# Products with V in pairs of key tiles, a fused minimum that writes to its own PSUM bank, and small rows shared

## The chip, the cores and the metric

The kernel runs on one core of a Trainium2 chip. The metric is the device time of one execution, in microseconds (us). Its engines work in parallel, each on its own queue in program order, and wait for one another through semaphores: TensorE (PE; weight loads are listed apart, as PEld), VectorE (DVE), ScalarE (ACT), GpSimd (POOL) and SyncE (SP), which issues the DMAs here.

## The reference

A transformer layer over x of shape (4, 512, 512), in fp32:

```
q, k, v = x Wq', x Wk', x Wv'            # 32 query heads, 8 key/value heads, 16 wide
q, k    = rope(q), rope(k)
attn    = softmax(causal(q k' / 4))      # each key/value head serves 4 query heads
x1      = layernorm(x + (attn v) Wo')
W       = mean_w + mean(|w - mean_w|) * sign(w - mean_w)     # for w1, w2, w3
out     = layernorm(x1 + (silu(x1 W1') * (x1 W3')) W2')      # 1792 wide inside
```

## The kernel before, in words

Four batches are four sections of eight steps; a step works on one key/value head with its four query heads, a *group*. A fifth section has only the tail of the last batch's groups. Then comes the feed-forward part, a loop over pairs of weight tiles, which no edit touches. Each engine has its own written-out order of the same steps.

A step is pipelined over groups. In eleven units n = 0 to 10, TensorE does the first pass of the step's own group (`pass1`, line 1056: logits with queries on the partitions, into one of three PSUM banks), and VectorE takes from each the least of the negated, masked logits (`maxima`, line 820: one fused instruction per head and query tile, and an accumulator read; 16 pairs a group). That instruction also has an elementwise result, which nothing reads; it goes to the tile `masked` in SBUF, in bf16. GpSimd splits the maxima in three bf16 parts, TensorE transposes them (line 1063), and a DMA puts them as extra rows under the queries.

Two steps later the group has its second pass (`pass2`, lines 1073 and 1075: logits again, now with keys on the partitions, less the maximum and with the mask added; two PSUM banks), and ScalarE takes the exponential of each unit into `Pt` (line 609). Units 0 to 3 are key tile 0 (one head each, 512 queries), 4 to 7 tile 1 (384 queries), 8 and 9 tile 2 (two heads each, 256), unit 10 tile 3 (four heads, 128).

The products with V (`pv`, line 1083) take one key tile at a time: for each of four heads a matmul with 128 rows and 32 columns of stationary V, in its own quarter of the array's columns and of one PSUM bank, in fp32, which the chip runs as two instructions; so 8 matmuls a product and four products a group, all accumulating in the bank BANK_O. Their places: tile 0 behind unit 6 and tile 1 behind unit 9 of the group's second pass, tile 2 behind unit 0 and tile 3 behind unit 2 of the next step. `Pt` has two buffers; tile t uses buffer t % 2. So the exponentials of a tile wait until the product of two tiles before is done (`pv_done`, line 608), and for tile 0 that is tile 2 of the group before, behind unit 0 of the same step. ScalarE copies the finished sums out behind unit 4 (`o_copy`, line 616), and tile 0 of the next group waits for that copy.

Between the units stand pieces of other work in TensorE's order: projections of q, k and v in six of eight steps (behind units 3, 5, 7 and 8, lines 969 to 971), the output projection of the batch before, transposes. VectorE has the rope products, the copy of the transposed maxima, residuals and layernorm statistics in the same way; in the last step of a section ScalarE takes square roots for the layernorm between unit 7 and unit 8, which loads another table and then the exponential's again. SP issues its DMAs in a fixed order with waits.

Small tiles: `mkw` (zeros, then a causal mask block), `mp` (128 columns for the parts of the maxima, 48 in use), `den` and `inv` (softmax sums and their reciprocals), `onesf` (128 x 128 ones for one column sum ahead of the feed-forward part, line 1146).

Of the kernel before, what the change touches and what calls it, by code (L numbers as in the profile page):

```python
# [27 lines left out]
F32 = mybir.dt.float32  # L28
F32R = mybir.dt.float32r
BF16 = mybir.dt.bfloat16  # L30
# [128 lines left out]
def layer(nc, xt, x, wqkv, wo, wall, cos, sin, ident, identf, mask, out):  # L159
    with ExitStack() as top:  # L160
# [75 lines left out]
        asum = top.enter_context(nc.sbuf_tensor("asum", [P, 3, NCO], F32))  # L236
        few = top.enter_context(nc.sbuf_tensor("few", [P, 6, QT], F32))
        csum, coef, sd, mean, shift, rs = (few[:, n] for n in range(6))
        onesf = top.enter_context(nc.sbuf_tensor("onesf", [P, P], F32))
        bnst = top.enter_context(nc.sbuf_tensor("bnst", [P, QT, 6], F32))  # L240
        mv = top.enter_context(nc.sbuf_tensor("mv", [P, QT, 2], F32))

# [12 lines left out]
        with ExitStack() as ctx:  # L255
            def sb(name, shape, dt):
                return ctx.enter_context(nc.sbuf_tensor(name, shape, dt))
# [1 line left out]
            NC = NH * HD + 2 * NKV * HD  # L259
            NM = 3 * GH * QT  # L260
            woH, woL = sb("woH", [P, KT, D], F32R), sb("woL", [P, KT, D], F32R)
            idb, mkw = sb("idb", [P, P], BF16), sb("mkw", [P, S], BF16)
            mk = mkw[:, S - P:S]
            Oe = sb("Oe", [P, S], F32)
            Oc = sb("Oc", [P, KT, S], F32)
            den, inv = sb("den", [P, 2 * GH * S // P], F32), sb("inv", [P, 2 * GH * S // P], F32)
            Inv = sb("Inv", [P, S], F32)
            OH, OL = sb("OH", [P, KT, S], F32R), sb("OL", [P, KT, S], F32R)
            negM = sb("negM", [P, 2, GH, QT], F32)
            mp_all = sb("mp", [P, P], BF16)  # L270
            mp = mp_all[:, 0:NM].rearrange("p (a h t) -> p a h t", a=3, h=GH)
            mT = sb("mT", [NM, P], BF16)
            with ExitStack() as first:


                def sb1(name, shape, dt):
                    return first.enter_context(nc.sbuf_tensor(name, shape, dt))

                wqH, wqL = sb1("wqH", [P, KT, NC], F32R), sb1("wqL", [P, KT, NC], F32R)
                xH, xL = sb1("xH", [P, KT, S], F32R), sb1("xL", [P, KT, S], F32R)  # L280
                xraw = sb1("xraw", [P, 2, S], F32)
                cs, sn = sb1("cs", [P, S], F32), sb1("sn", [P, S], F32)
                vT = sb1("vT", [P, S], F32)
                masked = sb1("masked", [P, 3, S], BF16)
                rp = sb1("rp", [P, 2, S], F32)
                co = sb1("co", [P, 2, 2, 512], F32)
                parts = sb1("parts", [P, 3, S], BF16)
                Qs, Ks = sb1("Qs", [P, NH, S], BF16), sb1("Ks", [P, NKV, S], BF16)
                Pt = sb1("Pt", [P, 2, GH, S], F32)
                V = sb1("V", [P, QT, NKV, 2 * HD], F32)  # L290
            XH, XL = sb("XH", [P, KT, B, S], F32R), sb("XL", [P, KT, B, S], F32R)

# [25 lines left out]
            with nc.Block() as block:  # L318
# [235 lines left out]
                def _(act):  # L554
# [48 lines left out]
                    def exp_unit(g, n):  # L603
                        t, h, m = U2[n]
                        w = S - P * t
                        act.wait_ge(p2_done, g[0] * NU + n + 1)
                        if h == 0:
                            act.wait_ge(pv_done, g[0] * QT + t + 1)
                        act.activation(Pt[:, t % 2, h:h + m, P * t:S],  # L609
                                       PS[:, BANK_P2 + (g[1] * NU + n) % 2, 0:m * w].rearrange("p (m w) -> p m w", m=m),  # L610
                                       ACT.Exp, scale=SCALE).then_inc(exped, 1)

                    def o_copy(g):
                        act.wait_ge(pv_done, g[0] * QT + QT + 2)
                        act.wait_ge(o_kept, g[0] * 16 + 16)
                        act.activation(Oe[:], PS[:, BANK_O, :], ACT.Copy).then_inc(o_out, 1)

# [71 lines left out]
                def _(dve):  # L689
# [124 lines left out]
                    def maxima(g, n):  # L814
                        t, h, m = U1[n]
                        w = P * (t + 1)
                        dve.wait_ge(p1_done, g[0] * NU + n + 1)
                        for i in range(m):
                            bank = PS[:, BANKS_P1[(g[1] * NU + n) % 3], i * w:(i + 1) * w]
                            least = dve.tensor_tensor_reduce(masked[:, (g[1] * NU + n) % 3, i * w:(i + 1) * w], bank,  # L820
                                                             mkw[:, S - w:S], -1.0, -MASKED,
                                                             ALU.add, ALU.min, negM[:, g[1] % 2, h + i, t:t + 1])
                        least.then_inc(p1_free, 1)

# [113 lines left out]

                    dve.memset(V[:], 1.0).then_inc(ready0, 1)
                    dve.memset(Ks[:], 1.0).then_inc(ready0, 1)  # L940
                    dve.memset(mp_all[:], 0.0).then_inc(ready0, 1)
                    dve.memset(onesf[:], 1.0).then_inc(ready0, 1)
                    dve.memset(mkw[:, 0:S - P], 0.0)
                    for ring in (g_free, exped, pv_done, co_abs, h_out):
                        dve.sem_inc(ring, 2)
                    for ring, free in ((p1_free, 3), (o_out, 1), (o_norm, 1), (o_kept, 16), (max_in, 16), (o_split, 4),
                                       (y_free, 16)):
                        dve.sem_inc(ring, free)
                    for k in range(KT):
# [16 lines left out]
                def _(pe):  # L966
# [93 lines left out]
                    def max_transpose(g, use):  # L1060
                        pe.wait_ge(max_split, g[0] + 1)
                        pe.wait_ge(g_free, use[0] + 1)
                        pe.transpose(g_bank(use[1]).bitcast(BF16)[:, 0:P], mp_all[:], idb[:]).then_inc(g_done, 1)

                    def pass2(g, n):
                        t, h0, m = U2[n]
# [8 lines left out]
                            last = pe.matmul(bank[:, i * w:i * w + P], mk, idb[:], start=False, stop=True)  # L1075
                        last.then_inc(p2_done, 1)

                    def pv(g, t):
                        if t == 0:
                            pe.wait_ge(o_out, g[0] + 1)  # L1080
                        pe.wait_ge(exped, g[0] * NU + LAST2[t] + 3)
                        for h in range(GH):
                            last = pe.matmul(PS[32 * h:32 * (h + 1), BANK_O, P * t:S], V[:, t, g[1], :],  # L1083
                                             Pt[:, t % 2, h, P * t:S], start=(t == 0), stop=(t == QT - 1),
                                             tile_position=(0, 32 * h))
                        last.then_inc(pv_done, 1)

                    def project_out(b, t, use, k):
                        if k == 0:
# [9 lines left out]
                    def section(sec):  # L1099
                        b = sec.b  # L1100
                        for st in range(NKV):
# [10 lines left out]
                            for n in range(NU):  # L1112
                                if g1:
                                    pass1(g1, n)
                                if g2:
                                    pass2(g2, n)
                                if n == 0 and g3:
                                    pv(g3, 2)
                                if n == 2 and g3:
                                    pv(g3, 3)  # L1120
                                if n in PROJECT_AT and up:
                                    tile, who = PROJECT[st]
                                    project(b + (who == "nxt"), tile, up, PROJECT_AT.index(n))
                                if not sec.cur and st < 2 and n in (2, 4, 6, 8):
                                    m = 4 * st + n // 2 - 1
                                    if m == 0:
                                        pe.wait_ge(p1_free, B * NKV * NU + 3)
                                        pe.wait_ge(x1_out, (B - 1) * QT)
                                    turn_early(m)
                                if n == 6 and g2:  # L1130
                                    pv(g2, 0)
                                if n == 9 and g2:
                                    pv(g2, 1)
                                if n == 9 and sec.use("turn", st):
                                    v_use = sec.use("project", 0)[0]
                                    turn(TURN[st], sec.use("turn", st), v_use)
                                if out_use:
                                    for k in ({1: (0,), 2: (1,), 3: (2, 3)} if st == 7 else {7: (0,), 9: (1,), 10: (2, 3)}
                                              ).get(n, ()):
                                        project_out(b - 1, st - OUT_STEP, out_use, k)  # L1140
                                if n == 3 and sec.use("max", st):
                                    max_transpose(sec.behind(st, 1), sec.use("max", st))
                            if not sec.cur and st == 1:
                                pe.wait_ge(fchain, 1)
                                pe.wait_ge(t_out, 2 * KT)
                                pe.matmul(PS[:, 0, 0:3], onesf[:], csum[:, 0:3], start=True, stop=True).then_inc(coef_ps, 1)
                            if not sec.cur and st == 2:
                                pe.wait_ge(coef_out, 1)
                                for n in range(2 * KT, 3 * KT):
# [74 lines left out]
```

## Time and profile before

| | us |
|---|---|
| three runs | 999.96, 1001.02, 1001.56 (median 1001.02) |
| the profiled execution, its own time | 1000.05 |
| its span, first to last instruction | 998.2 |
| attention: the products with V, first to last start | 75.3 to 494.8 |
| feed-forward, the steady stretch | 540 to 985 |

The profile is of one execution. A line of its groups gives busy time and the mean duration of one instruction; the span of a matmul overlaps its neighbour's, so the pace is read from start to start. `x8` stands for eight merged instructions. Idle time in brackets is that in front of an instruction on its engine, with what ended it.

### The profile page before, as it was taken

To read this page: it belongs to the slowest core of one execution; us is meant where nothing else is said; L and a number is where in the kernel's file an instruction comes from. 1 tells how busy PE (TensorE), PEld (TensorE's weight loads), DVE (VectorE), ACT (ScalarE), POOL (GpSimd) and SP (SyncE) were. 2 spreads that over 40 slices of the span, in tenths; PEclk is the share of its full clock that TensorE was granted. 3 is DMA by queue.
4 is the path that set the end of the run, shared out by engine and by line. 5 is a ranking of instruction groups with operands and counts; after the bars stand their busy time and mean duration, and the time that the engine had idled before them with its cause. 6 is when DMAs were issued, how large, how long until landed. Compare 5 with 4: busy or idle time off the path is not lost.

```text
span 998.2 us, 15539 instructions
## 1 busy us (share of the span) xinstructions
PE 906.2 (91%) x5186; PEld 609.8 (61%) x5186; DVE 720.9 (72%) x1896; ACT 356.5 (36%) x681; POOL 259.7 (26%) x323
## 2 busy tenths in 40 slices
PE   4379989899999989999897999999999999999993
PEld 2134435455444545444475888888888888888882
DVE  7587756767676767767467678777877787778777
ACT  0126756655765565655822011111111111111133
POOL 2046444754356432421333010111011101110000
PEclk9579989999998999999998999999999999999997
DMA  5757776754567541511341010111101110110004
GB/s 173 99 159 166 215 191 217 180 153 122 140 175 186 147 98 54 108 54 45 119 149 64 1 64 15 49 63 63 43 20 63 63 63 0 63 63 0 1 11 158
DMA packets 49692, 95.28 MB, mean 95 GB/s; under 512 B 11424, under 2 KB 25760, under 8 KB 48608
## 3 DMA queue, kind: packets, MB, share of 16 engines
q1 hardware_dynamic: 49632, 94.53, 33.7%
q8 instruction: 32, 0.52, 0.2%
q14 instruction: 28, 0.23, 0.1%
HBM read 66.72 MB, written 14.02 MB: 81 GB/s over the span
## 4 chain that ended last, share of the span: by engine, by line
PE 73%; DVE 10%; DMA 5%; issue 3%; ACT 3%; SPq 3%; POOL 2%; ACTq 0%; DVEq 0%; POOLq 0%
PE PS L969 19%; PE PS L970 18%; PE PS L971 18%; PE PS L1083 6%; PE PS L1056 5%; PE PS L1073 5%; DVE masked L820 3%; DMA Qs<-parts 2%; PE PS L1075 2%; DMA o_dram<-Oe 1%; SPq L349 1%; ACT Pt L609 1%; POOL xL L497 1%; DVE y L724 1%; DVE rp L812 1%
## 5 line engine op out<-in xcount | busy, mean ns | idle before, releaser
L820 DVE CUSTOM_DVE_ANT_0 masked<-PS,mkw 128x384 bf16<-128x384 f32 (+3 forms) x512 | 230.3, 485 | 111.7 <-PE PS L1056 108.4
L609 ACT ACTIVATE Pt<-PS 128x512 f32<-128x512 f32 (+1 forms) x352 | 192.0, 561 | 146.1 <-PE PS L1075 121.9
L969 PE MATMUL PS<-XH,WH 128*128 128x512 f32 x448 | 176.4, 394 | 3.8 <-DVE XL L774 3.8
L970 PE MATMUL PS<-XL,WH 128*128 128x512 f32 x448 | 176.1, 393 | 0.0
L971 PE MATMUL PS<-XH,WL 128*128 128x512 f32 x448 | 175.7, 392 | 0.0
L562 ACT ACTIVATE sg<-PS 128x512 f32<-128x512 f32 x56 | 33.6, 600 | 384.3 <-PE PS L971 384.3
L1056 PE MATMUL PS<-Ks,Qs 96*128 96x384 bf16 (+3 forms) x512 | 135.4, 319 | 28.0 <-DMA Qs<-parts 15.0
L1073 PE MATMUL PS<-Qs,Ks 99*128 99x256 bf16 (+3 forms) x512 | 142.7, 312 | 14.9 <-ACT Pt L609 12.2
L724 DVE TENSOR_TENSOR y<-PS,y 128x512 f32<-128x512 f32 x224 | 138.8, 682 | 0.0
L469 POOL TENSOR_TENSOR Wr<-Wr 128x512 f32<-128x512 f32 x42 | 54.5, 1326 | 319.0 <-DMA Wr<-wall 319.0
L1056 PEld LDWEIGHTS PS<-Ks,Qs 96*128 96x128 bf16 x512 | 42.8, 101 | 127.1 <-DVE negM L820 68.9
L1083 PE MATMUL PS<-Pt,V 128*32 128x512 f32 (+3 forms) x1024 | 101.6, 470 | 0.8 <-ACT Pt L609 0.3
L1075 PE MATMUL PS<-idb,mkw 128*128 128x128 bf16 x512 | 101.9, 224 | 0.0
L969 PEld LDWEIGHTS PS<-XH,WH 128*128 128x128 f32 x448 | 85.0, 190 | 22.2 <-DVE XL L774 4.4
L970 PEld LDWEIGHTS PS<-XL,WH 128*128 128x128 f32 x448 | 85.1, 190 | 17.7
L971 PEld LDWEIGHTS PS<-XH,WL 128*128 128x128 f32 x448 | 85.1, 190 | 17.7
L713 DVE TENSOR_TENSOR hf<-PS,hb 128x512 f32<-128x512 f32 x56 | 38.7, 692 | 71.7 <-PE PS L971 71.6
L969 PE MATMUL PS<-WH,hH 128*128 128x512 f32 x224 | 87.4, 390 | 2.0 <-issue 1.1
L971 PE MATMUL PS<-WH,hL 128*128 128x512 f32 x224 | 87.3, 390 | 0.0
L970 PE MATMUL PS<-WL,hH 128*128 128x512 f32 x224 | 87.2, 390 | 0.0
L502 POOL TENSOR_TENSOR co<-co 128x512 f32<-128x512 f32 x42 | 54.2, 1292 | 67.5 <-DMA co<-wall 67.4
L1073 PEld LDWEIGHTS PS<-Qs,Ks 99*128 99x128 bf16 x512 | 51.4, 101 | 33.0 <-ACT Pt L609 26.5
(101 smaller groups left out, 1228.7 us busy)
## 6 DMA issues: line engine op xcount, KB each, us to landing
co<-wall SPq DMA_DIRECT2D x42, 512.0 KB, 5.3
Wr<-wall SPq DMA_DIRECT2D x42, 512.0 KB, 4.8
Qs<-parts SPq DMA_DIRECT2D x96, 128.0 KB, 3.9
o_dram<-Oe SPq DMA_DIRECT2D x32, 256.0 KB, 2.8
xraw<-xt SPq DMA_DIRECT2D x16, 256.0 KB, 4.1
Oc<-o_dram SPq DMA_DIRECT2D x16, 256.0 KB
y<-x SPq DMA_DIRECT2D x4, 1024.0 KB, 8.9
Inv<-inv_dram SPq DMA_DIRECT2D x16, 256.0 KB
```

Source lines behind the costliest of these rows:

```text
L469: pool.tensor_tensor(w[:, 0], w[:, 0], w[:, 1], ALU.subtract).then_inc(w_diff, 1)
L502: pool.tensor_tensor(co[:, c % 2, 0], co[:, c % 2, 0], co[:, c % 2, 1], ALU.subtract).then_inc(co_diff, 1)
L609: act.activation(Pt[:, t % 2, h:h + m, P * t:S], PS[:, BANK_P2 + (g[1] * NU + n) % 2, 0:m * w].rearrange("p (m w) -> p m w", m=m), ACT.Exp ...
L724: dve.tensor_tensor(yt, PS[:, BANK_Y + t, :], yt, ALU.add).then_inc(y_free, 1)
L820: least = dve.tensor_tensor_reduce(masked[:, (g[1] * NU + n) % 3, i * w:(i + 1) * w], bank, mkw[:, S - w:S], -1.0, -MASKED, ALU.add, ALU.m ...
L969: pe.matmul(dst, stH, moH, start=(k == 0), stop=False)
L970: pe.matmul(dst, stH, moL, start=False, stop=False)
L971: return pe.matmul(dst, stL, moH, start=False, stop=(k == n - 1))
L1056: last = pe.matmul(bank[:, i * w:(i + 1) * w], Qs[0:ROWS, GH * g[1] + h0 + i, P * t:P * (t + 1)], Ks[0:ROWS, g[1], 0:w], start=True, stop= ...
L1073: pe.matmul(bank[:, i * w:(i + 1) * w], Ks[0:ROWS + 3, g[1], P * t:P * (t + 1)], Qs[0:ROWS + 3, GH * g[1] + h0 + i, P * t:S], start=True, ...
L1075: last = pe.matmul(bank[:, i * w:i * w + P], mk, idb[:], start=False, stop=True)
L1083: last = pe.matmul(PS[32 * h:32 * (h + 1), BANK_O, P * t:S], V[:, t, g[1], :], Pt[:, t % 2, h, P * t:S], start=(t == 0), stop=(t == QT - 1 ...
```

## The change

- `pv` takes two key tiles a call: tiles 0 and 1 behind unit 9, tiles 2 and 3 behind unit 2 of the next step. It waits once, for the last exponential of the second tile.
- `Pt` becomes four buffers, one per key tile, as wide as the tile needs. The exponentials of a tile now wait for the product of the same tile in the group before (`pv_done` starts at 4 in place of 2).
- The fused minimum writes its elementwise result back to the PSUM columns that it reads, as fp32; `masked` is gone.
- `inv` is `den`: the reciprocal is taken in place. `mp` and `mkw` share one row `row`, cleared by one memset (two before). `onesf` is one column, read 128 times over.

```diff
-        onesf = top.enter_context(nc.sbuf_tensor("onesf", [P, P], F32))
+        onesf = top.enter_context(nc.sbuf_tensor("onesf", [P, 1], F32))
...
-            idb, mkw = sb("idb", [P, P], BF16), sb("mkw", [P, S], BF16)
+            idb, row = sb("idb", [P, P], BF16), sb("row", [P, NM + S], BF16)
+            mp_all, mkw = row[:, 0:P], row[:, NM:NM + S]
...
-            den, inv = sb("den", [P, 2 * GH * S // P], F32), sb("inv", [P, 2 * GH * S // P], F32)
+            den = sb("den", [P, 2 * GH * S // P], F32)
+            inv = den
...
-                masked = sb1("masked", [P, 3, S], BF16)
...
-                Pt = sb1("Pt", [P, 2, GH, S], F32)
+                Pt = [sb1(f"Pt{t}", [P, GH, S - P * t], F32) for t in range(QT)]
...
-                        act.activation(Pt[:, t % 2, h:h + m, P * t:S],
+                        act.activation(Pt[t][:, h:h + m, :],
...
-                        act.wait_ge(pv_done, g[0] * QT + QT + 2)
+                        act.wait_ge(pv_done, g[0] * QT + 2 * QT)
...
-                            least = dve.tensor_tensor_reduce(masked[:, (g[1] * NU + n) % 3, i * w:(i + 1) * w], bank,
-                                                             mkw[:, S - w:S], -1.0, -MASKED,
+                            least = dve.tensor_tensor_reduce(bank, bank, mkw[:, S - w:S], -1.0, -MASKED,
                                                              ALU.add, ALU.min, negM[:, g[1] % 2, h + i, t:t + 1])
...
-                    dve.memset(mp_all[:], 0.0).then_inc(ready0, 1)
+                    dve.memset(row[:, 0:NM + S - P], 0.0).then_inc(ready0, 1)
                     dve.memset(onesf[:], 1.0).then_inc(ready0, 1)
-                    dve.memset(mkw[:, 0:S - P], 0.0)
-                    for ring in (g_free, exped, pv_done, co_abs, h_out):
+                    for ring in (g_free, exped, co_abs, h_out):
...
-                    def pv(g, t):
-                        if t == 0:
+                    def pv(g, t0):
+                        if t0 == 0:
                             pe.wait_ge(o_out, g[0] + 1)
-                        pe.wait_ge(exped, g[0] * NU + LAST2[t] + 3)
-                        for h in range(GH):
-                            last = pe.matmul(PS[32 * h:32 * (h + 1), BANK_O, P * t:S], V[:, t, g[1], :],
-                                             Pt[:, t % 2, h, P * t:S], start=(t == 0), stop=(t == QT - 1),
-                                             tile_position=(0, 32 * h))
-                        last.then_inc(pv_done, 1)
+                        pe.wait_ge(exped, g[0] * NU + LAST2[t0 + 1] + 3)
+                        for t in (t0, t0 + 1):
+                            for h in range(GH):
+                                last = pe.matmul(PS[32 * h:32 * (h + 1), BANK_O, P * t:S], V[:, t, g[1], :],
+                                                 Pt[t][:, h, :], start=(t == 0), stop=(t == QT - 1),
+                                                 tile_position=(0, 32 * h))
+                            last.then_inc(pv_done, 1)
...
-                                if n == 0 and g3:
+                                if n == 2 and g3:
                                     pv(g3, 2)
-                                if n == 2 and g3:
-                                    pv(g3, 3)
...
-                                if n == 6 and g2:
+                                if n == 9 and g2:
                                     pv(g2, 0)
-                                if n == 9 and g2:
-                                    pv(g2, 1)
...
-                                pe.matmul(PS[:, 0, 0:3], onesf[:], csum[:, 0:3], start=True, stop=True).then_inc(coef_ps, 1)
+                                pe.matmul(PS[:, 0, 0:3], onesf[:].broadcast_to([P, P]), csum[:, 0:3], start=True, stop=True).then_inc(coef_ps, 1)
```

## Rows read from the trace of the kernel before

**Rows 1.** The page: busy us, share of the span and instructions of each engine.

```profile
PE 906.2 (91%) x5186; PEld 609.8 (61%) x5186; DVE 720.9 (72%) x1896; ACT 356.5 (36%) x681; POOL 259.7 (26%) x323
```

**Rows 2.** The chain of waits that ended last: shares of the span by line.

```profile
by line: PE PS L969 18.6%; PE PS L970 17.7%; PE PS L971 17.7%; PE PS L1083 6.3%; PE PS L1056 5.3%; PE PS L1073 4.7%; issue 3.1%; DVE masked L820 2.7%; DMA Qs<-parts 2.2%; PE PS L1075 1.9%; DMA o_dram<-Oe 1.2%; SPq L349 1.1%; ACT Pt L609 1.0
```

**Rows 3.** Windows: stretch, length; busy of PE, PEld, DVE, ACT, POOL; clock, DMA, GB/s.

```profile
179.00:291.00 112.00, 104.71 (x772) 53.55 (x768) 79.39 (x305) 70.23 (x142) 56.70 (x74) 0.97 0.60 154
...
540.00:985.00 445.00, 439.53 (x1928) 362.99 (x1928) 336.26 (x568) 61.74 (x104) 42.10 (x35) 0.99 0.11 40
```

**Rows 4.** Timeline of PE around three products: start us, us, instruction.

```profile
203.36 0.22 PE L1075 MATMUL PS<-idb,mkw 128*128 128x128 bf16 x1
203.42 0.33 PE L1056 MATMUL PS<-Ks,Qs 96*128 96x384 bf16 x1
...
204.91 0.22 PE L1075 MATMUL PS<-idb,mkw 128*128 128x128 bf16 x1
205.06 1.07 PE L1083 MATMUL PS<-Pt,V 128*32 128x512 f32 x8
206.06 0.39 PE L1056 MATMUL PS<-Ks,Qs 96*128 96x512 bf16 x1
...
210.16 0.85 PE L1083 MATMUL PS<-Pt,V 128*32 128x384 f32 x8
210.95 0.49 PE L969 MATMUL PS<-woH,OH 128*128 128x512 f32 x1
...
229.58 0.64 PE L1083 MATMUL PS<-Pt,V 128*32 128x256 f32 x8
230.15 0.39 PE L1056 MATMUL PS<-Ks,Qs 96*128 96x256 bf16 x2
```

**Rows 5.** Timeline of the weight loads of one product, merged.

```profile
205.06 0.16 PEld L1083 LDWEIGHTS PS<-Pt,V 128*32 128x32 f32 x8 [0.21 <-issue]
```

**Rows 6.** The page's groups: count, busy us, mean ns, idle before and its releaser.

```profile
L820 DVE CUSTOM_DVE_ANT_0 masked<-PS,mkw 128x384 bf16<-128x384 f32 (+3 forms) x512 | 230.3, 485 | 111.7 <-PE PS L1056 108.4
...
L1083 PE MATMUL PS<-Pt,V 128*32 128x512 f32 (+3 forms) x1024 | 101.6, 470 | 0.8 <-ACT Pt L609 0.3
```

**Rows 7.** Waits of the whole span: total us, times, longest.

```profile
ACT Pt L609 <- PE PS L1083: 21.4, 16, 4.0
```

**Rows 8.** Timeline behind the product of tile 2 at 229.58, PE and ACT.

```profile
230.35 1.74 ACT L609 ACTIVATE Pt<-PS 128x512 f32<-128x512 f32 x3 [1.42 <-PE PS L1083]
...
230.38 0.38 PE L1073 MATMUL PS<-Qs,Ks 99*128 99x512 bf16 x1
...
230.66 0.38 PE L1056 MATMUL PS<-Ks,Qs 96*128 96x256 bf16 x2
...
231.00 0.39 PE L1073 MATMUL PS<-Qs,Ks 99*128 99x512 bf16 x1
```

**Rows 9.** Timeline of DVE and of ACT at unit 7, behind tile 0's product.

```profile
236.85 0.69 DVE L820 CUSTOM_DVE_ANT_0 masked<-PS,mkw 128x512 bf16<-128x512 f32 x1 [0.87 <-PE PS L1056]
...
237.08 0.49 ACT L609 ACTIVATE Pt<-PS 128x384 f32<-128x384 f32 x1 [1.05 <-PE PS L1075]
```

**Rows 10.** Timeline of PE in front of unit 10's second pass, a section's last step.

```profile
258.48 0.23 PE L1073 MATMUL PS<-Qs,Ks 99*128 99x128 bf16 x1 [1.77 <-ACT Pt L609]
```

**Rows 11.** Groups by line and shape of VectorE: busy us, mean ns, idle before.

```profile
L820 DVE CUSTOM_DVE_ANT_0 masked<-PS,mkw 128x512 bf16<-128x512 f32 x128 | 87.3, 690 | 77.8 <-PE PS L1056 76.2
...
L700 DVE SCALAR_TENSOR_TENSOR Wr<-Wr,few 128x512 f32<-128x512 f32 x42 | 32.3, 768 | 0.0
...
L820 DVE CUSTOM_DVE_ANT_0 masked<-PS,mkw 128x128 bf16<-128x128 f32 x128 | 29.5, 287 | 11.9 <-PE PS L1056 11.8
...
L808 DVE TENSOR_TENSOR rp<-PS,cs 128x512 f32<-128x512 f32 x20 | 13.8, 688 | 5.0 <-DMA Qs<-wo 2.6 <-POOL parts L493 2.2
...
L862 DVE TENSOR_TENSOR rp<-rp,parts 128x512 f32<-128x512 f32 x3 | 2.1, 693 | 9.5 <-ACT parts L597 9.5
```

**Rows 12.** Timeline of VectorE at the start: the memsets of mp and mkw.

```profile
6.18 0.11 DVE L941 MEMSET mp<- 128x64 uint32 x1
...
6.42 0.22 DVE L943 MEMSET mkw<- 128x192 uint32 x1
```

More of the change, by code:

```diff
@@ L269, in layer @@
             negM = sb("negM", [P, 2, GH, QT], F32)
-            mp_all = sb("mp", [P, P], BF16)
             mp = mp_all[:, 0:NM].rearrange("p (a h t) -> p a h t", a=3, h=GH)
@@ L940, in _ @@
                     dve.memset(Ks[:], 1.0).then_inc(ready0, 1)
-                    dve.memset(mp_all[:], 0.0).then_inc(ready0, 1)
+                    dve.memset(row[:, 0:NM + S - P], 0.0).then_inc(ready0, 1)
                     dve.memset(onesf[:], 1.0).then_inc(ready0, 1)
-                    dve.memset(mkw[:, 0:S - P], 0.0)
-                    for ring in (g_free, exped, pv_done, co_abs, h_out):
+                    for ring in (g_free, exped, co_abs, h_out):
                         dve.sem_inc(ring, 2)
-                    for ring, free in ((p1_free, 3), (o_out, 1), (o_norm, 1), (o_kept, 16), (max_in, 16), (o_split, 4),
+                    for ring, free in ((p1_free, 3), (pv_done, QT), (o_out, 1), (o_norm, 1), (o_kept, 16), (max_in, 16), (o_split, 4),
                                        (y_free, 16)):
@@ L1062, in max_transpose @@
                         pe.wait_ge(g_free, use[0] + 1)
-                        pe.transpose(g_bank(use[1]).bitcast(BF16)[:, 0:P], mp_all[:], idb[:]).then_inc(g_done, 1)
+                        pe.transpose(g_bank(use[1]).bitcast(BF16)[:, 0:P], mp_all, idb[:]).then_inc(g_done, 1)
                     def pass2(g, n):
```

## The prediction

> **What bounds the kernel now.** I read the engine totals first: TensorE is busy 91% of the span, VectorE 72% [rows 1]. Then the chain of work that ended last, by line: the feed-forward matmuls carry over half of it, and the products with V (line 1083) 6.3% [rows 2], or 62.9 of 998.2 us. Then the busy time by stage [rows 3]. In the feed-forward stretch (540 to 985 us) TensorE is busy 439.5 of 445 us, and the diff has no edit there, so that stage stays. In the steady attention stretch (179 to 291 us) TensorE is busy 104.7 of 112 us, VectorE 79.4, ScalarE 70.2. What the change is worth is decided in attention: 32 groups of heads, one group to a step.
>
> The order of TensorE's work shows what such a step loses. A product with V uses 32 of the array's columns, all other matmuls 128. Between neighbours of the 128-column kind the next matmul starts 0.06 us after one of 128 columns (203.36 to 203.42); in front of a product it takes 0.15 us (204.91 to 205.06) [rows 4]. From a product's start to the start of whatever follows it takes 1.00 us for 512 query columns, 0.79 for 384 and 0.57 for 256 [rows 4]. Those differ by 0.21 and 0.22 per 128 columns, so four times 0.213 leaves 0.15 us that does not depend on the columns. The fixed price of one product is so 0.15 + (0.15 - 0.06) = 0.24 us. There are 1024 such matmuls [rows 6], 8 to a product: 128 products, four to a group.
>
> **The pairs.** The change issues the products of key tiles 0 and 1 together behind unit 9, and those of tiles 2 and 3 together behind unit 2 of the next step. 64 of the 128 entries from and exits to the 128-column kind go. What a second product costs right behind a first no row shows. At best all of its fixed part goes (0.24 us saved). At worst only the entry goes and it keeps its own 0.15 us (0.09 saved). I take 0.18, nearer the best, because the eight weight loads of a product all lie within 0.16 us from its start [rows 5], while its first matmuls are streaming, so the second product's loads should find cover too.
>
> The Trainium skill (TensorE: Matmul & The Clock Gate, Part 3) says that a weight load overlaps running matmuls only where their row groups differ, and these products all use the same 128 rows. By that rule the saving would be the 0.09 us of the worst case and the whole sum 4 us smaller. The eight loads inside 0.16 us, under matmuls of the same rows, speak against it here.
>
> 64 x 0.18 = 11.5 us of TensorE time. Not all of it sets the end. Four products of a group take 1.00 + 0.79 + 0.57 + 0.36 (the last by the same slope) = 2.72 us, 87.0 us in 32 groups, and 62.9 of these are on the chain: 72%. 11.5 x 0.72 = **8.3 us gained**.
>
> **The four exponential buffers.** Two buffers became four, one per key tile, so the first exponential of a step no longer waits for the third product of the group before. In the trace ScalarE waits for products 16 times, 21.4 us in all [rows 7]. Its visible price on TensorE: in the step at 229 us the exponential starts at 230.35, released by the product, and unit 2's second pass then comes 0.34 us after its pair of 256-column matmuls (230.66 to 231.00), where the same pair in front took 0.23 (230.15 to 230.38) [rows 4, 8]. That is 0.11 us, 16 times: **1.8 us gained**. Upper bound 21.4 us, lower bound nothing (the buffer wait goes, the unit then waits for the exponential itself). I take 1.8, since units 1 and 2 offer about as much TensorE work as one exponential lasts.
>
> **What the moves bring forward.** Taking tile 0's product from behind unit 6 makes units 7 to 9 reach their waits 1.00 us earlier. Queued behind such a wait on TensorE are the rest of the unit, the projection matmuls and the pair itself; VectorE's maxima and ScalarE's exponentials wait for these. There is room: in front of unit 7 VectorE idles 0.87 us and ScalarE 1.05 us, both for TensorE [rows 9], so both would simply start earlier. In the last step of a section ScalarE ends the wait instead: TensorE stands 1.77 us for an exponential [rows 10]; the moved product fits into that gap. Three such gaps of up to 1.00 us against perhaps one step per section (four of them) in which unit 9 waits out the whole 1.00 us: +3 against -4 us, which I set at nothing. After the last batch there are two steps with second passes only; there the pair stands ahead of the last unit and holds up an exponential by at most the 0.79 us of tile 1. I take 0.65 twice: **1.3 us lost**. Moving tile 2's product by two units costs nothing: ScalarE's copy of the sums comes behind unit 4, later than both products. No DMA is issued elsewhere, and SP's and POOL's queues keep their order.
>
> **The minimum's result in its own bank.** 512 fused instructions, 485 ns mean [rows 6], now write 4-byte results to PSUM in place of 2-byte ones to SBUF. No VectorE row writes to PSUM. From the rows: reading PSUM or SBUF is alike for a two-operand instruction (688 and 693 ns for 512 columns), and the dearest two-operand form of that size takes 768 ns against 690 of ours [rows 11]. So a fixed extra lies between -5 and +78 ns; the far end is a rate halved by reading and writing one bank, (690 - 287) / 384 = 1.05 ns more for each of a mean of 320 columns [rows 11]: +336 ns. I take nothing, nearest to the 688/693 pair. What hides a small extra is VectorE's own idle time (0.87 us in front of unit 7).
>
> The Trainium skill (VectorE: DVE Perf Modes, The TRN2 errata) prices a VectorE instruction's fixed part at 58 cycles between SBUF operands and 120 with a PSUM source. If a PSUM destination cost the same 62 cycles, an estimate by that page is 512 x 65 ns = 33 us of VectorE time; for the source the 688 and 693 ns contradict it.
>
> **The small rows.** Shared rows, an in-place reciprocal and a one-column constant change no instruction in a loop. One memset less at the start, 0.1 to 0.2 us [rows 12], is in no term: nothing.
>
> **Sum.** 8.3 + 1.8 - 1.3 = 8.8 us. The profiled execution took 1000.05 us (span 998.2): 991.25. The median of the runs lies 0.97 us above it, 1001.02, so the forecast is **992.2 us**. By the bounds of the pair (0.09 and 0.24 us, 72%) it is 996.3 and 989.4; with all 64 on the path and the other gains, about 986.
>
> **Rivals.**
> 1. The savings only make TensorE reach its waits earlier. For it: an eighth of the steady stretch, one step, is 14.0 us, and VectorE is busy 9.9 of them [rows 3], with waits in both directions. Against it: TensorE is 93% busy there, and the two engines idle for it. A pair that keeps all of its fixed price belongs here: the change then does not do what it says. 997 to 1003 us.
> 2. A fixed extra of 78 ns on each minimum. 512 x 78 = 40 us of VectorE; the chain's share of that line is about a tenth (2.7% of 998.2 = 27 us [rows 2], of 230 [rows 6]), so 4 us at least, and 12 where units 3 to 6 of each step run out of slack: 996 to 1004 us.
> 3. The other side: reading and writing one bank halves the rate. 16 instructions of a step cost 16 x 0.336 = 5.4 us more, VectorE needs 15.3 of 14.0 us and becomes the bound; at the 93% which TensorE reaches now a step is 16.5 us, +2.5, and 32 of them +80: about 1072 us with the other gains. It decides from (14.0 - 9.9) / 16 = 0.26 us per instruction. Against it: nothing but the lack of a row.
> 4. More than the sum: the earlier units also shorten the ScalarE waits at the ends of sections. 980 to 985 us.
>
> **Chances.** Forecast 0.46 (its own range 986 to 997), rival 1 0.22, rival 2 0.15, rival 3 0.11, rival 4 0.06. A measurement of this kernel can tell 0.2%, or 2 us, from no change. Faster: 0.46 + 0.06, half of rival 1 (0.10), a quarter of rival 2 (0.04) = 0.66. Slower: rival 3, half of rival 2 and a little of rival 1 = 0.19. Same: 0.15. The range 985 to 1003 leaves out rival 3 and the ends of 2 and 4, under 0.2.
>
> **What would show it.** Pairs of tiles 0 and 1 that take 1.70 us from their start to the start of what follows (1.64 where all of the fixed price goes, 1.79 where only the entry does), pairs of tiles 2 and 3 that take 0.84; ScalarE's waits for products near zero; VectorE's minimum still 690 ns at 512 columns; the gap in front of unit 10 at the end of a section shorter; the steady stretch about 2.5 us shorter. A minimum over 0.26 us longer, or as much waiting for VectorE and ScalarE as the switches gave back, would prove it wrong.

## The result and the profile after

The changed kernel took 1008.17 us (median of four runs, 1006.44 to 1012.28) against 1001.16 for the kernel before beside it: ratio 1.0072, 95% interval 1.0053 to 1.0092. It is 7 us slower; the prediction was 992.2. The profiled run is the slowest of the four, 1012.28 us.

The engine totals answer to [rows 1]: TensorE is busy 4.5 us less, VectorE 18 us more. The 4.5 us are not the work saved, because the mean granted clock of TensorE was 0.952 here and 0.956 in the profile before.

```profile
PE 901.7 (89%) x5186; PEld 621.4 (61%) x5186; DVE 739.0 (73%) x1895; ACT 353.0 (35%) x681; POOL 258.1 (26%) x323
```

The same two windows as [rows 3]: the feed-forward stretch is as before; in attention TensorE's busy time fell by 3.3 us and VectorE's rose by 2.3. The window holds less of TensorE's work now (743 matmuls are listed, 772 before), so the 3.3 us are no saving either. From step start to step start the third section, eight steps, takes 112.92 us (112.77 before), and not about 2.5 us less, as was forecast for a stretch of that length. TensorE's granted clock was 0.5, the lower of its two levels (1.2 GHz), for 3.4 us of that section, and for 10.3 us before.

```profile
179.00:291.00 112.00, 101.43 (x743) 54.97 (x747) 81.70 (x303) 68.69 (x142) 57.31 (x73) 0.95 0.57 149
540.00:985.00 445.00, 440.26 (x1938) 364.14 (x1937) 336.60 (x556) 60.77 (x103) 46.61 (x38) 0.99 0.11 39
```

A pair of tiles 0 and 1 on TensorE (start, us):

```profile
247.70 0.22 PE L1073 MATMUL PS<-idb,row 128*128 128x128 bf16 x1
247.85 1.71 PE L1082 MATMUL PS<-Pt,V 128*32 128x512 f32 x16
249.49 0.50 PE L967 MATMUL PS<-woH,OH 128*128 128x512 f32 x1
```

and its weight loads, answering to [rows 5]:

```profile
247.85 0.16 PEld L1082 LDWEIGHTS PS<-Pt,V 128*32 128x32 f32 x8 [0.16 <-issue]
248.31 0.13 PEld L1082 LDWEIGHTS PS<-Pt,V 128*32 128x32 f32 x4 [0.30 <-issue]
248.74 0.13 PEld L1082 LDWEIGHTS PS<-Pt,V 128*32 128x32 f32 x4 [0.30 <-issue]
```

From its start to what follows, the pair takes 1.64 us (also the median of 27 at full clock); pairs of tiles 2 and 3 take 0.79. 1.64 is the prediction's figure for "all of the fixed price goes"; the 0.79 is below its 0.84, and 0.14 less than 0.57 + 0.36. The second product's eight loads lie under the first one's stream. The Trainium skill (TensorE: Matmul & The Clock Gate, Part 3) has a line that lets a load overlap running matmuls only where the row groups differ; these rows, with all loads and matmuls on the same 128 rows, contradict that line. (The paragraph at the head of the same part also lets a load go ahead when it targets the background weight buffer; whether that is so here, no row tells.) So the pairs did their part; the loss is elsewhere.

The minimum by shape (busy us, mean ns, idle before), in the changed kernel, for [rows 11]:

```profile
L820 DVE CUSTOM_DVE_ANT_0 PS<-PS,row 128x512 f32<-128x512 f32 x128 | 89.6, 708 | 66.8 <-PE PS L1054 66.4
L820 DVE DVE_READ_ACCUMULATOR2_ANT negM<- 128x1 f32 x512 | 71.0, 139 | 0.4
...
L820 DVE CUSTOM_DVE_ANT_0 PS<-PS,row 128x128 f32<-128x128 f32 x128 | 33.4, 323 | 9.0 <-PE PS L1054 8.8
```

and the accumulator's read in the kernel before, which the prediction did not look at:

```profile
L820 DVE DVE_READ_ACCUMULATOR2_ANT negM<- 128x1 f32 x512 | 42.1, 82 | 0.0
```

18 ns more at 512 columns, 36 at 128, and 57 on each read behind it. From the start of one minimum to the start of the next it is 0.249 us in place of 0.212 at 128 columns, 0.382 in place of 0.345 at 256.

TensorE's wait of the second pass for exponentials (total us, times, longest) in the kernel before:

```profile
PE PS L1073 <- ACT Pt L609: 12.2, 14, 1.8
```

and in the changed one:

```profile
PE PS L1071 <- ACT Pt L609: 19.3, 35, 1.4
```

ScalarE's waits for products [rows 7] are gone, and a new wait has come in their place, at the start of a step. In the first step of a section ScalarE has two row updates of y in front of its first exponential. The changed kernel there, TensorE and ScalarE:

```profile
382.37 1.51 ACT L672 ACTIVATE y<-y,few 128x512 f32<-128x512 f32 x2
...
383.16 0.38 PE L1054 MATMUL PS<-Ks,Qs 96*128 96x256 bf16 x2
...
383.78 1.72 ACT L609 ACTIVATE Pt<-PS 128x512 f32<-128x512 f32 x3
...
384.41 0.39 PE L1071 MATMUL PS<-Qs,Ks 99*128 99x512 bf16 x1 [0.87 <-ACT Pt L609]
...
384.79 0.86 PE L1082 MATMUL PS<-Pt,V 128*32 128x256 f32 x16
```

Unit 2's second pass needs the bank that the first exponential empties. The pair, whose operands had long been there, is queued behind that waiting pass, so TensorE stands idle with 0.8 us of work it could do. Before, tile 2's product lay behind unit 0, in front of this wait. The last step of a section has the same on VectorE: the output projection at unit 1 waits for a bank which VectorE frees by L812, behind four maxima. Before:

```profile
357.39 0.64 PE L1083 MATMUL PS<-Pt,V 128*32 128x256 f32 x8
...
358.93 0.50 PE L969 MATMUL PS<-woH,OH 128*128 128x512 f32 x1 [0.29 <-DVE rp L812]
```

After:

```profile
367.97 0.22 PE L1073 MATMUL PS<-idb,row 128*128 128x128 bf16 x1
369.33 0.50 PE L967 MATMUL PS<-woH,OH 128*128 128x512 f32 x1 [1.14 <-DVE rp L812]
```

The wait grew from 0.29 to 1.14 us: the product that stood in front of it is gone. The dearer minima have 0.17 us of this; with their result in SBUF (e2 below) the wait is 0.97.

### The profile page after: what moved, and what is told of

It reads as the page before. It is cut to its first block, busy times and chain, and to the rows that moved or that the text cites. A ratio compares the mean times of both kernels' runs of the same rounds, so it can differ in the third digit from the quotient of the medians.

```text
span 1010.5 us, 15538 instructions
## 1 busy us (share of the span) xinstructions
PE 901.7 (89%) x5186; PEld 621.4 (61%) x5186; DVE 739.0 (73%) x1895; ACT 353.0 (35%) x681; POOL 258.1 (26%) x323
## 4 chain that ended last, share of the span: by engine, by line
PE 68%; DVE 12%; DMA 8%; issue 5%; SPq 3%; ACT 3%; POOL 1%; ACTq 0%; DVEq 0%; POOLq 0%
PE PS L967 18%; PE PS L969 17%; PE PS L968 17%; PE PS L1082 5%; PE PS L1054 4%; PE PS L1071 4%; DVE PS L820 3%; DMA Qs<-parts 2%; PE PS L1073 2%; DMA o_dram<-Oe 2%; SPq L349 2%; DMA Qs<-mT 1%; DMA xraw<-xt 1%; ACT Pt L609 1%; DVE negM L820 1%
## 5 line engine op out<-in xcount | busy, mean ns | idle before, releaser
L820 DVE CUSTOM_DVE_ANT_0 PS<-PS,row 128x384 f32<-128x384 f32 (+3 forms) x512 | 241.3, 512 | 95.2 <-PE PS L1054 93.6
L1073 PE MATMUL PS<-idb,row 128*128 128x128 bf16 x512 | 103.0, 226 | 0.0
L1082 PE MATMUL PS<-Pt,V 128*32 128x512 f32 (+3 forms) x1024 | 88.2, 465 | 0.5 <-ACT Pt L609 0.5
L969 PE MATMUL PS<-WH,hL 128*128 128x512 f32 x224 | 87.3, 390 | 0.0
L820 DVE DVE_READ_ACCUMULATOR2_ANT negM<- 128x1 f32 x512 | 71.0, 139 | 0.4
```

The costliest lines, as they stand in the source:

```text
L820: least = dve.tensor_tensor_reduce(bank, bank, mkw[:, S - w:S], -1.0, -MASKED, ALU.add, ALU.min, negM[:, g[1] % 2, h + i, t:t + 1])
L969: return pe.matmul(dst, stL, moH, start=False, stop=(k == n - 1))
```

## Experiments

Two theories. **O** (order): the late pair's place behind unit 2 costs, because TensorE now reaches the waits at a step's start with nothing to do in front of them. **P** (PSUM): the dearer minimum costs. "On the changed kernel" or "on the kernel before" says what each edit starts from. Ratios are to runs of the kernel before beside each experiment, and differences between two experiments go by their ratios.

**e1: the kernel before, with the minimum's result in its own bank.**

```
-  least = dve.tensor_tensor_reduce(masked[:, ... % 3, ...], bank, mkw[...], ...)
+  least = dve.tensor_tensor_reduce(bank, bank, mkw[...], ...)
```

> The kernel before with one edit: the fused minimum writes its elementwise result to its own bank. Theory P (the slower minimum costs the time): its start-to-start spacing grows by 37 ns at 128 and 256 columns and by 5 to 30 ns above, the accumulator read takes 139 ns, and since VectorE's chain at the start of a step sets the projection, the kernel takes 8 to 15 us more (1009 to 1016). Theory O (the moved products cost the time): the minimum is slower but VectorE's idle time hides most of it, 0 to 4 us more (1001 to 1005).

1005.88 us, ratio 1.0033 (1.0008 to 1.0058); 704 and 324 ns at 512 and 128 columns, the read 139. Between the two expectations: the PSUM result alone costs 0.33%, about half of the 0.72% lost, though the interval allows 0.1 to 0.6%.

**e2: the changed kernel, with the minimum's result in SBUF again** (two slots and a wait on VectorE's own earlier work, the fourth exponential buffer laid over the second, to make room, with the waits that this needs).

```
+  masked = sb1("masked", [P, 2, S], BF16)
+  Pt.append(Pt[1][:, :, 0:P])
...
+  dve.wait_ge(p1_free, g[0] * NU + n + 2)
-  least = dve.tensor_tensor_reduce(bank, bank, ...)
+  least = dve.tensor_tensor_reduce(masked[:, (g[1] * NU + n) % 2, ...], bank, ...)
```

> The changed kernel with the minimum's result in SBUF again (two slots in place of three, with a wait of VectorE for its own unit two before; the fourth exponential buffer lies in the second, which is free by then). Theory P: without the slow minimum the pairs' 64 x 0.23 = 14.7 us show, 986 to 992. Theory O: unit 2's second pass still waits 0.6 us for the first exponential in about 16 steps (10 us), so the pairs bring little: 996 to 1003.

1002.79, ratio 1.0007 (0.9983 to 1.0032), the minimum back at 689, 286 and 82 ns. Taking P's price away gives back 0.65% but leaves nothing of the pairs' gain. P alone falls.

**e3: the changed kernel, with the late pair behind unit 1.**

```
-  if n == 2 and g3:
+  if n == 1 and g3:
       pv(g3, 2)
```

> The changed kernel with the pair of tiles 2 and 3 behind unit 1 in place of unit 2, so that it stands in front of unit 2's second pass. Theory O: the 0.6 us waits of that pass for the exponential go, 995 to 1000. Theory P: the VectorE chain decides, 1004 to 1009.

998.75, ratio 0.9967 (0.9948 to 0.9985): one number in the order is worth 10.5 us. The second pass's wait:

```profile
PE PS L1071 <- ACT Pt L609: 8.9, 19, 1.5
```

The first step of a section in e3 shows why:

```profile
370.72 1.51 ACT L672 ACTIVATE y<-y,few 128x512 f32<-128x512 f32 x2
...
371.60 0.86 PE L1082 MATMUL PS<-Pt,V 128*32 128x256 f32 x16
...
372.13 2.21 ACT L609 ACTIVATE Pt<-PS 128x512 f32<-128x512 f32 x4
...
372.39 0.39 PE L1054 MATMUL PS<-Ks,Qs 96*128 96x256 bf16 x2
372.77 0.39 PE L1071 MATMUL PS<-Qs,Ks 99*128 99x512 bf16 x1
```

The row updates are as long, but the pair runs beside them, and the second pass starts without a wait. In the last step the projection's wait for L812 is 0.35 in place of 1.14.

**e4: both edits, e2 and e3.**

> Both: the minimum's result in SBUF, and the pair of tiles 2 and 3 behind unit 1. If the two losses are separate and these are all, the pairs' gain is left: 985 to 991. If it stays above 996, a third loss is open (the pair of tiles 0 and 1 behind unit 9).

992.80, ratio 0.9915 (0.9884 to 0.9946), six runs: faster than both kernels, and near what the prediction gave the change, though by other terms (see the account below). Its mean granted clock was 0.957 against 0.954 beside it, worth 1.5 us (below), so 0.993 is the safer figure.

**e5: the buffers without the pairs** (e2 with the four products one by one at their old places).

```
-  if n == 2 and g3:
-      pv(g3, 2)
+  if n in (0, 2) and g3:
+      pv(g3, 2 + n // 2, False)
...
-  if n == 9 and g2:
-      pv(g2, 0)
+  if n in (6, 9) and g2:
+      pv(g2, n // 9, False)
```

> The change without its pairs and without its PSUM result: four exponential buffers (the fourth laid over the second), the result of the minimum in SBUF in two slots, and the four products of a group one by one at their old places (behind units 0, 2, 6 and 9). Theory O (what the change gains are the 64 removed switches, what it loses is the place of the late pair): the buffers alone are worth at most the 1.8 us that the prediction gave them, so 0 to 2 us below the kernel before, and the second pass's wait for the exponential stays short (about 12 us in all). Rival B (the four buffers are themselves what gains, or what loses, and the pairs are worth little): 3 us or more to either side of the kernel before.

1001.89, ratio 1.0002 (0.9986 to 1.0018). The buffers are worth nothing by themselves. The wait is 12.5 us (14 times), as before: without the wait for the product, the second pass waits for the exponential itself.

**e6: only the pair of tiles 0 and 1** (e5 with the second edit left out).

> The kernel of e5 with one thing more: tiles 0 and 1 as a pair behind unit 9; tiles 2 and 3 stay separate behind units 0 and 2. 32 of the 64 switches of column tiling go, at 0.23 us each 7.4 us of TensorE time. Theory O: with tile 2's product still behind unit 0 nothing is given back, so 4 to 7 us below e5. Rival (the work taken from behind unit 6 opens a wait of its own, or pairs only reach waits earlier): within 2 us of e5.

999.24, ratio 0.9970 (0.9953 to 0.9986): 3 us of the 7.4 that its 32 switches are worth, under the expected 4 to 7. That is more than the rival's 2 us, but the intervals do not exclude it. The mean granted clock was 0.952 against 0.954, worth under 1 us, so that it may be nearer 4. From here, pairing tiles 2 and 3 behind unit 1 (e4) takes off 0.55%, behind unit 2 (e2) it adds 0.37%: the same saved switches with either sign.

**e7: e4 with the early pair behind unit 10.**

```
-  if n == 9 and g2:
+  if n == 10 and g2:
       pv(g2, 0)
```

> The kernel of e4 (SBUF result, pair of tiles 2 and 3 behind unit 1) with the pair of tiles 0 and 1 one unit later, behind unit 10, the last of a step. Theory O says that a pair is best where TensorE would otherwise wait for a chain on ScalarE; the next step's first exponential is made to wait by unit 10's exponential and the sum of absolute values, so a pair in that place should cover the wait: 0 to 3 us below e4's ratio of 0.9915. Rival: unit 10's second pass then stands ahead of the pair and nothing is left to cover, or the o_copy chain behind it comes later: 0 to 4 us above it.

1002.78, ratio 1.0016 (1.0001 to 1.0031): a miss, and not a clean one, for two reasons. First, more changed than the place: the fourth exponential buffer lies over the second, so unit 10's exponential must wait for tile 1's product, which now stands behind unit 10's second pass. ScalarE has a wait that e4 does not have (total us, times, longest):

```profile
ACT Pt L611 <- PE PS L1086: 71.4, 30, 4.6
```

Second, its mean granted clock was 0.943 against 0.954 for the kernel before beside it, and by the scatter of those runs (below) that is 4 to 5 us of the 10 lost against e4. Steps 5 and 6, at full clock, are no longer than e4's (14.83 and 14.83 us). The last steps of the second and third sections are: 16.94 and 17.22 us against 13.97 and 13.97, with 3.4 and 6.6 us of them at half the clock and e4's at the full one. Why the clock was granted less is open, and the place behind unit 10 stays untested by itself.

**e8: the changed kernel, with ScalarE's sum of absolute values one unit earlier.**

```
-  if n in (8, 10) and sec.nxt and st < NCO // 2:
-      abs_sum(b, 2 * st + (n == 10))
+  if n in (8, 9) and sec.nxt and st < NCO // 2:
+      abs_sum(b, 2 * st + (n == 9))
```

> The changed kernel with one edit: ScalarE's sum of absolute values, which stands behind unit 10's exponential and so ahead of the next step's first exponential, moves in front of unit 10's exponential (behind unit 9). Everything else is as changed, the late pair behind unit 2 and the PSUM result included. Theory O (the second pass of unit 2 waits for the first exponential, which waits for the exponential of unit 10 and the sum of absolute values in front of it): 4 to 9 us below the changed kernel, and the wait of the second pass for the exponential falls from 19 us towards 10. Rival (the pair's own place costs, whatever stands on ScalarE; moving the sum only delays unit 10's exponential by as much): within 2 us of the changed kernel.

1005.91, ratio 1.0029 (1.0010 to 1.0049): 4.3 us below the changed kernel, at the edge of what was expected; the wait's total hardly moved (18.9 us, 25 times). In step 4 of a section (steps counted from 0) the changed kernel has

```profile
321.06 0.62 ACT L620 ACTIVATE co<-co 128x512 f32<-128x512 f32 x1
...
321.68 1.72 ACT L609 ACTIVATE Pt<-PS 128x512 f32<-128x512 f32 x3
...
322.32 0.39 PE L1071 MATMUL PS<-Qs,Ks 99*128 99x512 bf16 x1 [0.43 <-ACT Pt L609]
```

and e8 has the first exponential and unit 2's second pass without it:

```profile
318.52 2.24 ACT L609 ACTIVATE Pt<-PS 128x512 f32<-128x512 f32 x4 [1.60 <-PE PS L1073]
...
319.68 0.38 PE L1071 MATMUL PS<-Qs,Ks 99*128 99x512 bf16 x1
```

So the sum of absolute values is one of the things that stand in front, but the smaller part of the loss. Its price is seen best in step 1, which holds no half clock (behind the table of steps below).

**e9: the kernel before with 4-byte results of the minimum in SBUF** (two slots, the small rows shared).

```
-  masked = sb1("masked", [P, 3, S], BF16)
+  masked = sb1("masked", [P, 2, S], F32)
```

> The kernel before with the shared small rows and with one more edit: the minimum's elementwise result stays in SBUF but has 4 bytes an element instead of 2 (two slots, with a wait on the engine's own earlier work). It tells apart why the changed kernel's minimum is dearer. Theory place (a PSUM result is dearer): 690, 543, 420 and 287 ns at 512, 384, 256 and 128 columns as before, the read of the accumulator 82 ns, and a time within 2 us of the kernel before. Theory bytes (4-byte results are dearer wherever they go): the read 139 ns, 323 ns at 128 columns, and 2 to 5 us above the kernel before, as with the PSUM result alone.

1001.92, ratio 1.0007 (0.9985 to 1.0028). Its groups:

```profile
L822 DVE CUSTOM_DVE_ANT_0 masked<-PS,row 128x512 f32<-128x512 f32 x128 | 87.0, 690 | 72.8 <-PE PS L1057 71.2
...
L822 DVE DVE_READ_ACCUMULATOR2_ANT negM<- 128x1 f32 x512 | 42.0, 82 | 0.0
```

Not the bytes: PSUM as the place of the result makes the minimum dearer, at least where it writes over the columns that it reads; no run writes to another bank. The shared small rows, which this kernel has too, are worth nothing, as predicted.

**e10: e8 with the late pair behind unit 1 in a section's first and last step alone.**

```
-  if n == 2 and g3:
+  if n == (1 if st in (0, 7) else 2) and g3:
```

> The kernel of e8 (ScalarE's sum of absolute values one unit earlier, PSUM result, late pair behind unit 2) with the late pair behind unit 1 in two of a section's eight steps alone: the first, where ScalarE has two row updates of y in front of its first exponential, and the last, where the output projection at unit 1 waits for VectorE. In the other six it stays behind unit 2. Theory O in its full form (the late place costs only in steps where something stands in front of unit 2 at a step's start: the sum of absolute values, the row updates, the output projection): nearly the whole price of the late place goes, 8 to 11 us below the changed kernel, at e3's ratio of 0.9967 within 0.002. Rival (the place itself costs in every step): a quarter of what is left between e8 and e3, 1 to 3 us below e8's 1.0029.

999.34, ratio 0.9990 (0.9970 to 1.0011): 8.2 us below the changed kernel, 3.9 below e8. The place costs in those steps, not in every one. It stays 0.0023 above e3, just outside the 0.002 expected, with intervals that overlap.

The length of the steps, from one step's first first-pass matmul to the next one's, third section and the start of the fourth, shows it place by place (us; steps counted from 0, steps 3 and 4 together, of which step 3 has 3.4 or 6.8 us at half the clock in every row; * with about 3 us at half the clock):

```
                           3+4    5      6      7      0      1      2
before                    29.84  15.09  15.07  14.94  13.11* 12.11  12.59
changed                   30.64  15.11  15.11  15.15  12.15  11.64  12.68
e8  sum earlier           29.99  15.11  15.11  15.17  12.15  11.65  12.68
e10 and behind 1 in 0, 7  30.13  15.11  15.11  14.24  11.29  11.65  12.67
e3  behind 1 everywhere   29.59  15.13  15.11  14.24  11.31  11.64  12.67
e2  SBUF result           30.51  14.83  14.83  14.91  12.24  11.65  12.35
e4  SBUF, behind 1        30.09  14.83  14.83  13.97  11.41  11.64  12.36
e6  SBUF, pair 0, 1 only  29.55  14.83  14.83  14.47  11.81  11.75  12.35
```

Behind unit 2 costs 0.9 us in step 7 and 0.85 in step 0, nothing in steps 2, 5 and 6, and nothing in the step 1 shown, which is the fourth section's, where no sum of absolute values is taken. In the third section's step 1, where one stands in front of the first exponential, the changed kernel and e2 take 12.23 us, and e3, e4, e8 and e10 11.63 or 11.64, all at full clock: there the place costs 0.59 us, and moving the sum (e8) takes all of that away. The PSUM result costs 0.28 in steps 5 and 6 and 0.32 in step 2. Where in steps 5 and 6 is seen in their projection, which waits for VectorE's addition to y. Before:

```profile
329.44 0.69 DVE L841 TENSOR_TENSOR y<-PS,y 128x512 f32<-128x512 f32 x1
...
330.19 0.51 PE L969 MATMUL PS<-xH,wqH 128*128 128x512 f32 x1 [0.19 <-DVE y L841]
```

After:

```profile
339.88 0.69 DVE L840 TENSOR_TENSOR y<-PS,y 128x512 f32<-128x512 f32 x1
...
340.62 0.49 PE L967 MATMUL PS<-xH,wqH 128*128 128x512 f32 x1 [0.69 <-DVE y L840]
```

e2:

```profile
329.83 0.69 DVE L844 TENSOR_TENSOR y<-PS,y 128x512 f32<-128x512 f32 x1
...
330.57 0.50 PE L971 MATMUL PS<-xH,wqH 128*128 128x512 f32 x1 [0.41 <-DVE y L844]
```

These steps start at 326.63, 336.80 and 327.02, so the projection starts 3.56, 3.82 and 3.55 us into them. Its time is VectorE's: the late pair saves nothing here, it only lengthens the wait (0.19 to 0.41), and the dearer minima in front (four of 128 columns, two of 256) add 0.27.

## Why the prediction was wrong

**The pairs: right in kind, under-sized.** 0.18 us a pair was predicted, 0.23 came (0.14 to 0.15 between the products, 0.09 at the entry), 14.7 us of TensorE time for 11.5.

**The 72% that reaches the end: too high.** In e6, 3 to 4 of 7.4 us do; in e4, 7 to 8.5 of 14.7. The chain's share of the products [rows 2] tells where the old ones lay, not whether another engine's chain is due a little later, as in steps 5 and 6. Rival 1 was right there.

**The exponential buffers: nothing, not 1.8 us** (e5). The wait for the product went, as forecast, and the lower bound came true.

**The step that failed: "Moving tile 2's product by two units costs nothing: ScalarE's copy of the sums comes behind unit 4, later than both products."** It asked who waits for the product, and did not ask what the product covered on TensorE. With the claim that "units 1 and 2 offer about as much TensorE work as one exponential lasts" it left out what ScalarE does ahead of that exponential (the row updates, 1.4 us in step 0; the sum of absolute values) and the projection at unit 1 of step 7, which waits for VectorE. All of these are in the order of the code. Price: 10.5 us with the PSUM result (e3 against the changed kernel), 9.2 without (e4 against e2).

**The minimum's own bank: mis-sized.** Nothing was taken, from the 688/693 pair of rows, which shows the reading side. Measured: 0.037 us more from one minimum to the next at 128 and 256 columns and 0.06 to 0.1 to the end of its read, near the 78 ns of rival 2. Price: 0.33% on the kernel before (e1), 0.65% on the changed one (against e2), 0.52% with the late pair behind unit 1 (e3 against e4); the intervals overlap, so that it is dearer there is not shown. Rival 3, the halved rate, is refuted (708 ns at 512 columns). The Trainium skill (VectorE: DVE Perf Modes, The TRN2 errata) asks 62 cycles more for a PSUM source; the prediction's estimate from it for a PSUM destination was 65 ns, 33 us in all. The read's 57 ns, 29 us in all, are close to that estimate, closer than the nothing taken from the nearest rows. But the page speaks of a source, for which the 688 and 693 ns contradict it, so the agreement may be luck.

**The moves of tile 0's product** were set at nothing; no run separates them from the pair (e6 has both). The gap in front of unit 10 did go, as forecast: the 1.77 us of [rows 10] are in no run with the pair behind unit 9. The 1.3 us lost in the last steps did not come: from the start of the last step with a first pass to the first feed-forward matmul it is 41.85 us before and 41.61 in e4, both at full clock. Behind unit 2 (e8) it is 42.73.

In sum: e4's gain of 0.85%, the late place (0.92%) and the PSUM result (0.65%) make the 0.72% that was lost. They add up by construction, since each price is the difference between two of these kernels; only e1, e5 and e6 test the parts by themselves.

**What stays open.** The lengths of steps 3 and 4 depend on when a transfer lands (next section but one), so the 1.05 us a section between the changed kernel and e3 there is not shown to be all the order's. Nor is it shown, stage by stage, where the changed kernel lies behind the kernel before. Between the two profiled executions, 12.2 us apart, 6.4 us are in the first section, 2.9 in the second, 0.15 in the third and 2.1 from the last step with a first pass to the feed-forward part, and the changed kernel's whole span has 97.7 us at half the clock, the one before 87.3. The price of the place is seen directly, at full clock, in steps 0, 1 and 7; the rest is known from the times of whole runs.

## What to carry to other kernels

Independent work in an in-order queue is worth most where it stands in front of a wait. Before moving it, ask not only who waits for it but which wait it covers, and list everything that the releasing engine does ahead of that release, step kind by step kind. And price an instruction's output place by a row that writes there; if no row does, keep it at a bound, not at the value for the input side.

## What the runs showed of the hardware

A PSUM destination (the columns that it reads) costs VectorE's minimum 18 to 36 ns and the accumulator's read behind it 57 ns (82 to 139), whereas 4-byte results in SBUF cost nothing (690 and 82 ns).

Of two neighbouring products on 32 columns the second loads its weights under the first: the pair takes 1.64 us where the two apart take 1.00 + 0.79, and the 0.15 us in front of a product (0.06 between matmuls on 128 columns) is there once.

In step 4 of the third section TensorE does not set the length: a transfer into `co` lands, GpSimd subtracts, multiplies (L524), ScalarE splits (L658), and only then comes the exponential that TensorE waits for. In the changed kernel:

```profile
328.15 1.27 POOL L502 TENSOR_TENSOR co<-co 128x512 f32<-128x512 f32 x1 [3.92 <-DMA co<-wall]
329.39 1.27 POOL L524 TENSOR_TENSOR Oc<-Oc,Inv 128x512 f32<-128x512 f32 x1
...
330.69 0.63 ACT L658 ACTIVATE OH<-Oc 128x512 fp32r<-128x512 f32 x1 [3.20 <-POOL Oc L524]
...
331.76 0.28 PE L1071 MATMUL PS<-Qs,Ks 99*128 99x256 bf16 x1 [1.35 <-ACT Pt L609]
```

The multiplication started 7.12 to 9.01 us into that step in eight profiles (before, changed, e2, e3, e4, e6, e8, e10), and the step ended 7.39 to 7.42 us later in each (7.57 in e5, 6.95 in e1). It started late (8.61 to 9.01) where the granted clock was 0.5 for 3.4 us of step 3, and early (7.12 to 7.89) where it was 0.5 for 6.8 us. In the second section the two groups overlap (8.51 to 10.09 us with 3.4, 7.41 to 8.92 with 6.8). That fits transfers which go on while TensorE is slowed, but no run varies it alone, so it is not shown.

Runs of one kernel scatter with the mean granted clock: 29 runs of the kernel before, beside e1 to e4, go from 998.08 us at 0.960 to 1008.22 at 0.947, 0.47 us for each 0.001 by a straight line. Beside e5 to e8 it is 0.38 (34 runs, without one of 1012.51 us at 0.945). This says that the two go together, not which makes the other.
